# A third feed-forward of a transformer chain that computes only each token's two experts, on tokens sorted through DRAM

## The reference, cut to what matters

```
# FFN2: E = 8 experts, TOP_K = 2, D = 128, H = 256
logits = einsum('bsd,de->bse', x, Wg)
top_vals, top_idx = top_k(logits, 2)
probs = softmax(top_vals)
weights = einsum('bsk,bske->bse', probs, one_hot(top_idx, 8))
for e in range(8):
    u, v = x @ W1[e], x @ W2[e]
    out = out + (silu(u) * v) @ W3[e] * weights[..., e]
# ATTN3: xw = x @ W_in + b; gates from xw @ W_gx and xw @ W_ga; a recurrence along the tokens; @ W_out
# FFN3: 8 experts of one 128x128 matrix each, the two best of each token added without weights
```

## Time and profile before

| what | before |
|---|---|
| median of three runs | 1122.7 us |
| the profiled execution: its time | 1122.91 us |
| its span (first to last instruction) | 1121.1 us |
| PE busy | 980.5 us (87%) |
| DVE, ACT, POOL busy | 620.5, 521.6, 224.4 us |
| mean granted TensorE clock | 0.953 |
| chain that ended last, by engine | PE 67%, DVE 11%, issue 10%, ACT 6% |
| end of the scan of ATTN2 | 860.3 us |

### The profile page before, as it was taken

How to read it: one execution, slowest core, us unless ns; L and a number is a source line. 1 busy time by engine, 2 the same in 40 slices (tenths; PEclk the granted TensorE clock), 3 DMA queues, 4 the chain that set the end, 5 groups by cost and what they waited for, 6 DMA issues and landing times.

```text
span 1121.1 us, 11072 instructions
## 1 busy us (share of the span) xinstructions
PE 980.5 (87%) x3601; PEld 430.4 (38%) x3628; DVE 620.5 (55%) x1149; ACT 521.6 (47%) x902; POOL 224.4 (20%) x225
## 2 busy tenths in 40 slices
PE   5799999998799898988767966877778999999896
PEld 2345545454222222232234742322224444444343
DVE  2223232434788878775243444489997544545573
ACT  4233232233367667777532322666665424564540
POOL 9100000000001101100553660256662000000000
PEclk9799999999899999999879997989999999999998
DMA  8630000030022212200413106000000311110022
GB/s 178 188 111 0 1 1 1 14 79 0 23 64 54 60 46 69 56 25 4 111 47 82 48 24 188 11 0 1 1 1 1 100 52 48 47 38 19 8 107 75
DMA packets 70733, 55.50 MB, mean 50 GB/s; under 512 B 21912, under 2 KB 62158, under 8 KB 70581
## 3 DMA queue, kind: packets, MB, share of 16 engines
q1 hardware_dynamic: 66836, 51.26, 16.4%
q0 software_dynamic: 3840, 3.55, 1.1%
HBM read 41.65 MB, written 13.77 MB: 49 GB/s over the span
## 4 chain that ended last, share of the span: by engine, by line
PE 67%; DVE 11%; issue 10%; ACT 6%; POOL 2%; SPq 2%; DMA 1%; another core or an unknown queue 1%; DVEq 0%; POOLq 0%; ACTq 0%
PE psum L706 65%; ACT sb_scr L1673 3%; DVE sb_scr L2363 3%; DVE sb_scr L2733 2%; DVE sb_scr L2742 1%; ACT psum L1673 1%; POOL sb_scr L686 1%; ACT sb_qstack L1673 1%; SPq L535 1%; PE psum L862 1%; SPq L540 0%; DVE sb_scr L2225 0%; PE psum L1255 0%; DMA sb_scr<-pick_rows 0%
## 5 line engine op out<-in xcount | busy, mean ns | idle before, releaser
L1673 ACT ACTIVATE sb_scr<-psum 128x512 f32<-128x512 f32 (+6 forms) x564 | 306.3, 579 | 357.6 <-PE psum L706 274.4
L706 PE MATMUL psum<-sb_h,sb_wide 128*128 128x512 f32 x448 | 210.7, 599 | 0.8 <-ACT sb_scr L1673 0.8
L2363 DVE TENSOR_REDUCE sb_scr<-psum 128x2 f32<-128x1024 f32 x128 | 154.6, 1222 | 40.1 <-PE psum L706 40.0
L706 PE MATMUL psum<-sb_scr,sb_wide 128*128 128x512 f32 x256 | 125.6, 594 | 0.8 <-DVE sb_scr L2788 0.8
L706 PEld LDWEIGHTS psum<-sb_h,sb_wide 128*128 128x128 f32 x448 | 83.5, 193 | 93.3 <-issue 91.7
L647 POOL DMA_DIRECT2D sb_heads<-sb_scr x48 | 24.9, 525 | 440.1 <-DVE sb_scr L2379 439.8
L706 PE MATMUL psum<-sb_kstack,sb_qstack 96*128 96x512 bf16 x256 | 98.3, 395 | 11.4 <-DVE sb_scr L2363 8.5
L686 POOL TENSOR_TENSOR sb_scr<-sb_scr 128x512 f32<-128x512 f32 x64 | 83.1, 1305 | 91.5 <-ACT sb_scr L1673 45.8
L2289 DVE TENSOR_SCALAR sb_scr<-psum,sb_b 128x512 f32<-128x512 f32 x48 | 34.5, 747 | 116.9 <-PE psum L706 116.9
L1673 ACT ACTIVATE sb_scr<-psum,sb_b 128x512 f32<-128x512 f32 x48 | 31.3, 685 | 143.4 <-PE psum L706 143.4
L706 PE MATMUL psum<-sb_qstack,sb_kstack 128*128 128x512 bf16 x233 | 90.1, 392 | 4.8 <-ACT sb_scr L1673 3.3
(11 more groups left out here) (290 smaller groups left out, 1256.0 us busy)
## 6 DMA issues: line engine op xcount, KB each, us to landing
sb_scr<-weight_rows SPq DMA_DIRECT2D x32, 256.0 KB
sb_qstack<-q_bounce SPq DMA_DIRECT2D x48, 96.0 KB
sb_kstack<-k_bounce SPq DMA_DIRECT2D x144, 32.0 KB
sb_scr<-pick_rows SPq DMA_DIRECT2D x8, 512.0 KB
expert_in<-sb_scr SPq DMA_DIRECT2D x4, 645.0 KB, 6.0
sb_scr<-expert_in SPq DMA_DIRECT2D x8, 322.5 KB, 3.4
expert_out<-sb_scr SPq DMA_DIRECT2D x4, 512.0 KB, 4.8
sb_scr<-expert_out SPq DMA_DIRECT2D x8, 256.0 KB, 4.6
```

What stands on the lines that cost most here:

```text
L706: return nc.tensor.matmul(out_, w, r, start=start, stop=stop, **kw)
L1673: return nc.scalar.activation(out_, in_, func, **kw)
L2363: v.reduce_max(headmax[:, g % 2, t:t + 2, j], banks, AX.X).then_inc(sem("maxed"), 1)
```

## The change

FFN2 computes only the two experts that each token chose. The tokens are taken in two halves (batches 0, 1 and batches 2, 3). Of each half, 2048 (token, choice) rows are sorted by expert in DRAM (`tiles_in`), each expert's block rounded up to tiles of 128 rows, so that 23 tiles (2 x 8 + 7) always suffice: 46 tiles in all. For each tile PE turns the rows to columns (`turn_in2`), multiplies with the tile's rows as the stationary side and the expert's [W1 W2] (512 columns) as the moving side (`up2`), turns the 256 hidden values back (`turn_hidden2`), and multiplies with W3 (`down2`, two matmuls of 128x128). Which expert's weights are read is a register of PE's, loaded from SBUF (`block_of`, `value_load`): 23 loads ahead of the first half, one inside each tile's turn in the second. POOL scatters the 46 tiles of results to `tiles_out`, SP gathers them, DVE weighs and adds them (`combine2`), PE turns them back.

The routing of half 0 moves into the last 22 steps of the scan on DVE, PE, ACT and POOL (6 of its 16 scatters); that of half 1 stands at the start of the tile loop, and its 16 scatters on POOL between the scatters of results of tiles 3 to 10. ATTN3 now runs in pairs of batches: 0 and 1 beside the tiles of half 1, 2 and 3 behind the last tile, where FFN3's routing of batches 0 and 1 stands between its steps. At the start of the program five more DMAs clear `tiles_in`. The dense loop, `hidden2`, the second product and the 32 weight DMAs go.

```diff
+TILES2 = 2 * HT + E2 - 1
+NTILE2 = len(HALVES) * TILES2
...
+            for n, size in BLANKS:
+                sp.dma_start(tiles_in[n * P:(n + size) * P].rearrange("(p r) d -> p (r d)", p=P),
+                             blank[:, 0:size * ROW]).then_inc(sem("table_cleared"), 16)
...
+            def load_tile(c):
+                if c % TILES2 == 0:
+                    sp.wait_ge(sem("scattered"), 16 * (K1 * NT + K1 * HT * (c // TILES2 + 1)))
...
+            for c in range(NTILE2):
+                load_tile(c)
+                if c == TILES2 + X2_RING - 1:
+                    gather2(0)
+            gather2(1)
...
+            SCATTER_BESIDE = (5, 7, 9, 11, 13, 15)
...
+            for c in range(NTILE2):
+                if c + ROWS_AHEAD < NTILE2:
+                    know_rows(c + ROWS_AHEAD)
+                scatter_out(c)
+                if 3 <= c < 3 + HT:
+                    for k in range(K1):
+                        scatter_in(1, K1 * (c - 3) + k)
...
-                s0 = 2 * (n % UP2)
-                mm(bank(s0), w1_2[:, e, k * P:(k + 1) * P], h[:, b, :])
-                mm(bank(s0 + 1), w2_2[:, e, k * P:(k + 1) * P], h[:, b, :]).then_inc(sem("up2_done"), 1)
...
+                mm(bank(UP2_BANKS[c % 3]), xT2_in[:, c % 2, :], WIDE[:, bass.ds(blocks[c], 2 * H2)]).then_inc(sem("up2_done"), 1)
...
+            pe.wait_ge(setup, SETUP.index("tiles2_0") + 1)
+            for c in range(TILES2):
+                blocks[c] = block_of(c)
+            score2(1, 5)
+            turn_rows2(3, 6)
...
+            for c in range(NTILE2 + 2):
+                if c + 1 < NTILE2:
+                    if c + 1 == TILES2:
+                        pe.wait_ge(setup, SETUP.index("tiles2_1") + 1)
+                    if c + 1 >= TILES2:
+                        blocks[c + 1] = block_of(c + 1)
+                    turn_in2(c + 1)
+                if c < NTILE2:
+                    up2(c)
+                if 1 <= c < NTILE2 + 1:
+                    turn_hidden2(c - 1)
+                if c >= 2:
+                    down2(c - 2)
+                beside_tiles(c)
+
+            project_out3(0, 6)
+            project_out3(1, 7)
+            center4(0, 1)
+            center4(1, 2)
+            turn_back2(2, 6)
+            turn_back2(3, 7)
+            variance4(0, 3)
...
+                if n == 15:
+                    nc.scalar.preload_act_table_set(LOG_EXP)
+                    deviation3(0, 6)
+                    deviation3(1, 7)
+                    nc.scalar.preload_act_table_set(SILU_TANH)
...
+            def route_beside(i):
+                st = route2_steps[0]
+                if i == 42:
+                    take_scores2(0, 7)
+                    best2(0, st)
+                if i == 43:
+                    best_at2(0, st)
+                if i == 44:
+                    choose2(0, st)
+                if i == 47:
+                    place2(0, st, 7)
+                if i == 49:
+                    tile_experts2(0, st)
...
+            gate_input3(0)
+            gate_input3(1)
+            recur3(0)
+            recur3(1)
+            add_batch_attn3(0, 6)
+            add_batch_attn3(1, 7)
+            combine2(2)
+            combine2(3)
```

More of the change, by code:

```diff
@@ L230, in by_expert @@
+        routes2 = [Route2(half) for half in range(2)]
         def by_expert(at):
@@ new lines, in best_at2, with choose2 @@
+            def best_at2(half, st):
+                r = routes2[half]
+                st.wait()
+                v.tensor_tensor(r.gap, r.top[:, :, 1], r.top[:, :, 0], ALU.subtract).then_inc(setup, 1)
+                for t in range(HT):
+                    st.did(v.max_index(r.top_at[:, t, :], r.top[:, t, :], r.scores[:, t, :]))
+            def choose2(half, st):
+                r = routes2[half]
+                one_hot = r.one_hot.rearrange("p (n e) -> p n e", e=E2)
+                st.then(lambda: v.tensor_copy(r.expert_at.rearrange("p (k t) -> p k t", k=K1), r.top_at[:, :, 0:K1].rearrange("p t k -> p k t")))
+                st.then(lambda: v.tensor_tensor(one_hot, iota[:, 0:E2].unsqueeze(1).broadcast_to([P, K1 * HT, E2]),
+                                                r.expert_at.unsqueeze(2).broadcast_to([P, K1 * HT, E2]), ALU.is_equal))
+                st.wait()
+                v.tensor_tensor(r.chosen, r.one_hot[:, 0:HT * E2], r.one_hot[:, HT * E2:], ALU.add).then_inc(setup, 1)
@@ new lines, in tile_experts2 @@
+            def tile_experts2(half, st):
+                r = routes2[half]
+                st.did(v.tensor_tensor(r.passed[0:1], iota[0:1, 0:TILES2].unsqueeze(2).broadcast_to([1, TILES2, E2 - 1]),
+                                       r.ends[0:1, 0:E2 - 1].unsqueeze(1).broadcast_to([1, TILES2, E2 - 1]), ALU.is_ge))
+                st.then(lambda: v.reduce_sum(r.tile_expert[0:1], r.passed[0:1], AX.X))
+                st.wait()
+                st.end()
+                v.tensor_scalar(r.tile_block[0:1], r.tile_expert[0:1], float(BLOCK2), None, ALU.mult).then_inc(setup, 1)
@@ L2826, in _ @@
[L2826 to L2828 removed]
+            take_scores2(1, 5)
+            best2(1, st)
+            best_at2(1, st)
+            choose2(1, st)
             dve.wait_ge(sem("act_setup"), 7)
@@ L2897, in _, with beside_tiles @@
-            normalize4(2, 2)
+            def beside_tiles(c):
+                n = c - TILES2
+                if c == 2:
+                    place2(1, st, 7)
+                if c == 3:
+                    tile_experts2(1, st)
+                if c in (4, 6):
+                    weigh2(c // 2 - 2)
+                for b in range(2):
+                    at = 6 + b
+                    if n == 8 + b:
+                        combine2(b)
+                    if n == 10 + b:
+                        add_batch2(b, at)
+                    if n == 16 + b:
+                        normalize3(b)
```

783 lines of the change are left out of this document (453 added, 330 removed).

## The result

The changed kernel takes 1129.4 us (median of 20 runs, 1124.2 to 1134.0) against 1122.4 for the kernel before in the same set: ratio 1.0055, 95% interval 1.0035 to 1.0076. It is 0.55% slower, where 0.6% faster was forecast. In a later set of runs the same two kernels took 1104.8 and 1108.7 us: ratio 0.9946 (0.9912 to 0.9981). So the sign of the change depends on something outside the kernel, and most of what follows is about that.

What follows compares the result with a forecast made beforehand. DVE bounds the scan, PE's matmuls the dense FFN2. 860.3 + 6 + 23.3 + 49.8 + 68 + 107.3 = 1114.7 us of span, so 1116.5 us against 1122.7, 0.6% faster; range 1085 to 1146, the forecast's own 1100 to 1132.

Steps and rivals of the forecast that it cites:

- The scan, +6: End of ATTN2's scan: half 0's routing on DVE makes it end 6 us later, bounds 3 to 12.
- some twelve operations of 0.2 to 0.3: DVE's routing of half 0 in the scan: these, eight maxima and eight index searches, together 5.9 us.
- rival 3: Scan: POOL's products and six scatters hold DVE up more, +8 to +20 us, 1125 to 1137 us; chance 0.16.
- To the first tile, 23.3: Scan's end to first tile: PE's chain, with 23 register loads at 0.6 us, decides over POOL's; 23.3 us.
- Rivals 1 and 2: PE's register loads: nearly free (under 0.1 us), 1102 us, chance 0.24; or 1.3 us each, 1143 us, chance 0.16.
- hand-over of 1.3 us: POOL's scatters to SP's loads through DRAM: 1.3 us from the end of the issue, read from FFN1's rows.
- the 2.8 us that the prediction would add: Four hand-overs through DRAM: by the skill's page each 0.7 us longer, the sum 2.8 us higher; the rows were kept.
- Half 0, 49.8: First 23 tiles: PE needs 42.6 us, but POOL's scatters and copies set the half at 49.8 us.
- PE never waited at tile 23: Half 0, sign of being wrong; the forecast had PE idle 3 to 8 us ahead of tile 23.
- Half 1, 68: Second 23 tiles up to the last `up2`: tiles 42.6 us, ATTN3 matmuls and turns 9.6, stalls and loads; about 68.
- The tail, 107.3: From the last `up2` to the end: ATTN3 of batches 2 and 3, routing and FFN3; 107.3 us, before 64.
- (e): FFN3 at the tail's end: PE work 43 us, picks wait 6.3, slow clock 5, last matmul to end 4.7; 58.7.

Runs made afterwards that it cites:

- e4: Changed kernel, but the six scatters of half 0's rows between the scan's last steps stand behind it: 1125.4 us, 1.0022 of the kernel before.
- e1: Changed kernel, but only the first register load stands ahead of the tile loop, the other 22 inside it: 1117.6 us, 0.9965 of the kernel before.
- f1: The changed kernel itself, unaltered, run again in a later set on a chip where the kernel before took 1108.7 us: 1104.8 us, ratio 0.9946.
- e7: As e1, but in the tail four picked products of FFN3 and their matmuls go ahead of ATTN3's recurrence and projection: 1115.5 us, 0.9926 of the kernel before.

## Why the prediction was right or wrong, point by point

- *The scan, +6.* The mechanism was right (DVE sets the pace, the routing's cover is gone), the size was not: 11.9, within the bound of 12. The failed term is "some twelve operations of 0.2 to 0.3": five of them took 0.95 to 1.31 beside POOL's products. The count was short as well: even quiet the 40 operations are 6.7 us, not 5.9. The row that said so was in the earlier trace rows, and I had used it only for rival 3. I named POOL's scatters as a cause of the bound too; e4 shows that they cost nothing. Rival 3's range for the time, 1125 to 1137, is where the result lies, but only about half of the miss is its own.
- *To the first tile, 23.3.* 24.7. The loads at 0.62, and PE's chain ahead of POOL's, were right (e1). The scores and turns took 4.3 us where the sum had 2.4, the 16 score records 3.58 of them: behind the 14 us without work the granted clock was 0.50 from 892.5 to 896.9, the lower of its two levels (1.2 GHz). Rivals 1 and 2 fell. The sum's hand-over of 1.3 us counts from the end of a scatter's issue; from its start FFN1's rows show 2.25 (595.78 to 598.03), so the 2.8 us that the prediction would add to it do not follow from those rows.
- *Half 0, 49.8.* The step that failed on the first kind. POOL's queue was worked out rightly, three indirect DMAs and a copy per tile in 3.89 us (912.85 to 916.74) against 4.09, and on the second kind the half took 50.0. But I let PE run freely until tile 23, with its signals reaching DVE and ACT at once. On the first kind they came up to some 7 us late and PE was stopped from tile 6 on: 66.5 us. I had written that I would be wrong if PE never waited at tile 23: at 963.42 it did not wait (the 0.20 us there is its register load).
- *Half 1, 68.* 59.6, since in the longer half 0 POOL had caught up: tile 31 waited 0.96 us instead of 3, and the results of half 0 were there when DVE weighed them. On the second kind, where POOL is behind, 66.9. The two halves belong together: 126.1 us measured, 117.8 predicted, 117.0 on the second kind. A tile with its load took 1.96 us against 1.95 in the sum, and that was luck: the tile itself takes 1.67 and not 1.85, the load 0.30 and not 0.1.
- *The tail, 107.3.* 104.0. The first pick came 47.0 us behind the last `up2` (1070.01 against 1022.97), as written; `combine2` of batch 2 began behind ATTN3's adds (1038.45), as written. Nothing here failed, though the parts of (e) add up to 59.0, not 58.7.
- *The sum.* As a difference to the kernel before the forecast was -6.2 us; -3.9 was measured on the second kind of chip and +7.0 on the first. What lies between them is mostly the two halves, 9.1 us longer on the first kind; stage by stage it cannot be closed, since f1's profiled execution, 1110.7 us, is the slowest of its ten. The anchor was blind to it as well: the kernel before itself holds 14 us more on the first kind, and in the changed kernel, which shares the code up to there, all of the 14 come between 549 and 674 us, while POOL scatters FFN1's rows and results.

What stays open: what it is that holds PE's signals. It was seen only beside indirect DMAs that follow one another at 1.28 to 1.49 us on POOL; it did not come at 1.65 to 1.8 us, nor from a busy POOL, nor from 72 GB/s of tile loads and results; and it is there in some sets of runs and not in others. I call that a kind of chip, but two sets that bore the same chip number fell to different kinds, so it may belong to what surrounds it.

## What to carry to other kernels

Price an operation that moves under another engine's load by its rows under that load; the quiet duration is only the lower bound (0.29 against 1.31 us here). When a trace of before has waits with no releaser beside work that the change will double, find out what they are before the sum is made: the "remote" rows of FFN1 pointed at the stall of half 0. A chain of small loads costs its full latency where nothing is queued behind it; moving e1's loads was worth more than the change's whole deficit, and with POOL's scatters of the next half put ahead of the results of this one the kernel (with e1's and e7's changes in it) beat the one before on both kinds of chip, by 2.3 to 3.0% and by about 1%. And where a result is near 1%, the kernel before has to be run beside the new one in every set, and in more than one: here one set said slower and another faster.
